# Cross-attention and FP4 feed-forward: heads times values, then a projection of 256 rows, instead of values folded with the output weights

## The chip, the core and the metric

The kernel runs on one NeuronCore of a Trainium2 chip. The core has five engines with a queue each: TensorE (PE, matmuls and transposes into PSUM), VectorE (DVE), ScalarE (ACT), GpSimd (POOL) and SyncE (SP, which only issues DMAs here). An engine works through its queue in order, and waits on semaphores for the others. The metric is the device time in microseconds of one execution; a profiled execution gives the trace.

## What is computed

x is 2 x 1024 x 256, the context 2 x 154 x 256. A layer norm, cross-attention with 16 heads of 64, a layer norm and a gated feed-forward of width 704 whose weights and inputs are rounded to FP4 in blocks of 16:

```python
q = einsum('bnd,hdk->bhnk', layernorm(x), proj_q) + bias_q
k = einsum('bnd,hdk->bhnk', ctx, proj_k) + bias_k
v = einsum('bnd,hdv->bhnv', ctx, proj_v) + bias_v
attn = softmax(einsum('bhqk,bhnk->bhqn', q, k) / sqrt(64))
heads = einsum('bhqn,bhnv->bhqv', attn, v)
x = x + transpose(heads, (0, 2, 1, 3)).reshape(2, 1024, 1024) @ w_out.T
u = layernorm(x)
x = x + fp4_linear(silu(fp4_linear(u, w_gate)) * fp4_linear(u, w_up), w_down)
```

## The kernel before

A product is done with halves: each operand is a float16 `high` and the float16 rest, `low`, and `three` (L349) issues three matmuls, high x high, high x low and low x high. So nearly every PSUM tile that is to be an operand is rounded by ScalarE (high) and then subtracted by VectorE (low).

**Setup.** It loads and splits the projections, makes keys (`J_K` jobs), w_out transposed (`J_WO`) and values (`J_V`, `heads_out`), the latter as a block-diagonal matrix of head pairs, and then folds values with the output weights: 20 `J_VW` jobs (`fold`, evicted by `vw_high` and `vw_low` L870). The result `vw` has for each batch and each row of (head, context position), 16 x 154 = 2464 rows in 20 chunks of 128, the 256 output columns. Among these jobs stand the queries and scores of the first tile, the row statistics and the layer norm of tiles 1 to 7.

**Attention.** There are 8 steps; step i treats rows 128 i to 128 i + 127 of both batches, s = 0 and 1 being the batch. `attention(i)` is written for each engine as a loop over s and five slots g, and that order is the queue. In a slot TensorE scores four heads of the next tile (`score`, L443, for g below 4), transposes 512 columns of the probabilities of this tile (`turn_p`, L451, four fp32 transposes), does one of the side jobs (transposes of the next step's normalised x, L413; one of four query blocks `query(n, j)`, in slots 2 to 4 of the first tile and slot 1 of the second), and multiplies a transposed group with `vw` (`mix`, 12 matmuls of 256 columns, L351 to L353 from vw). VectorE does in a slot the row maximum (L925), the inverse of the row sums (L930), the low half of the transposed probabilities (L934), and the low half of a query (L916); ScalarE the exps (L672), the high half (L682) and that of a query (L663); GpSimd scales the probabilities (L1155). All query blocks from step 1 on share the PSUM bank `Q_BANK`, so a block waits for the low half of the one ahead (`q_low`). One group's mix of a tile into `O_BANK` starts when the sum of the tile before has been read (`x1_ready`). `add_attention` (L942) adds the tile's sum to xs and takes its statistics (L828).

In steps 0 to 5 a sixth of the FFN's weights is rounded to FP4 too: block scales (L951 to L955, second tile, slot 0, VectorE), values (L1161, L1163, GpSimd), magnitudes (L741, ScalarE, slot 3), two grid operations (L984, L986, VectorE, slot 4), and a last product on GpSimd (L1186). In step 7 the weights are transposed (`turn_weights`), and x of the first FFN step is quantised.

**FFN.** Eight steps of two tiles: gate and up (24 matmuls of 352 columns per tile), silu, hidden (L1072), quantising over VectorE, GpSimd and ScalarE, transposes, and the down projection. It is the same before and after.

## Time and profile before

| | us |
|---|---|
| median of 3 runs (454.4 to 455.08) | 454.61 |
| profiled execution | 453.78 |
| its span | 451.6 |
| start of step 1 of attention | 100.4 |
| steps 1 to 5, each | 30.08 |
| step 6 | 28.2 |
| step 7 up to the sum of its second tile | 23.6 |
| first FFN matmul | 302.67 |

The page gives busy times over the whole span. A step is best read in the windows (busy time of each engine in a stretch) and then in the timeline of one engine, where a bracket behind a row names what the engine waited for. The chain of waits follows the work that ended last back in time; where it changes the engine, one engine released the other. Step numbers are those of the loop; the boundaries in the windows are at VectorE's first row maximum of a step.

### The profile page before, as it was taken

What the parts mean: (1) busy time and instruction counts of PE and PEld (TensorE: products, weight loads), DVE (VectorE), ACT (ScalarE), POOL (GpSimd) and SP (SyncE); (2) the same over time, 40 slices, a digit from 0 to 9 for tenths busy, and PEclk for the clock granted to TensorE, in tenths of its full rate; (3) what the DMA queues carried; (4) which work ended last, traced back from release to release, by engine and by line L of the source; (5) the groups of instructions that cost most, each with busy time, mean ns of one, the idle gap of its engine ahead of it and who ended that gap; (6) DMA issues with size and microseconds to landing.
All of it is one profiled execution on the core that took longest, in us unless ns stands there. A gap on an engine that the chain in (4) does not pass through costs nothing.

```text
span 451.6 us, 9319 instructions
## 1 busy us (share of the span) xinstructions
PE 387.9 (86%) x3581; PEld 306.9 (68%) x3581; DVE 346.3 (77%) x677; ACT 277.4 (61%) x859; POOL 206.9 (46%) x183
## 2 busy tenths in 40 slices
PE   1889759999999999999999999996487797788955
PEld 1568638877878878778788788884256565566744
DVE  2789886777876687678766879778868998998792
ACT  3497757678777876787778767855224435424421
POOL 8250033263353442633535423513557778777841
PEclk9999988999999999999999999999888999999998
DMA  7960000000000000000000000000000000000011
GB/s 240 320 220 1 2 0 1 1 1 1 3 1 2 1 1 3 1 1 2 1 1 1 2 1 2 0 2 0 1 1 1 23 14 12 25 13 12 25 36 35
DMA packets 8426, 11.46 MB, mean 25 GB/s; under 512 B 499, under 2 KB 6335, under 8 KB 8383
## 3 DMA queue, kind: packets, MB, share of 16 engines
q1 hardware_dynamic: 8383, 10.88, 7.5%
q8 instruction: 28, 0.46, 0.4%
q14 instruction: 15, 0.12, 0.1%
HBM read 8.78 MB, written 2.10 MB: 24 GB/s over the span
## 4 chain that ended last, share of the span: by engine, by line
DVE 38%; PE 34%; POOL 10%; ACT 10%; issue 6%; DMA 1%; SPq 0%; POOLq 0%; ACTq 0%; DVEq 0%
PE ps L351 9%; PE ps L353 8%; PE ps L352 8%; POOL arena L1163 4%; PE ps L451 4%; PE ps L443 4%; DVE arena L934 4%; DVE negmax L925 3%; ACT arena L672 3%; DVE arena L984 3%; DVE arena L916 3%; DVE arena L986 3%; DVE vw L870 3%; DVE blk_h L951 2%; DVE arena L1072 2%
## 5 line engine op out<-in xcount | busy, mean ns | idle before, releaser
L1155 POOL TENSOR_TENSOR arena<-arena,rinv 128x616 f32<-128x616 f32 x64 | 77.6, 1213 | 148.6 <-DVE rinv L930 148.6
L351 PE MATMUL ps<-vw,arena 128*128 128x256 f16 (+1 forms) x352 | 98.0, 278 | 12.3 <-DVE arena L823 6.1
L672 ACT ACTIVATE arena<-ps,negmax 128x154 f32<-128x154 f32 x256 | 96.0, 397 | 18.0 <-DVE negmax L925 17.7
L352 PE MATMUL ps<-vw,arena 128*128 128x256 f16 (+1 forms) x352 | 97.8, 278 | 0.0
L353 PE MATMUL ps<-vw,arena 128*128 128x256 f16 (+1 forms) x352 | 97.7, 277 | 0.0
L934 DVE TENSOR_TENSOR arena<-ps,arena 128x512 f16<-128x512 f32 x80 | 54.9, 686 | 18.7 <-ACT arena L682 18.5
L682 ACT ACTIVATE arena<-ps 128x512 f16<-128x512 f32 x80 | 48.5, 606 | 25.2 <-PE ps L451 24.0
L351 PE MATMUL ps<-arena,xnT_h 128*128 128x352 f16 x128 | 41.2, 322 | 18.1 <-DVE xnT_l L994 16.3
L925 DVE TENSOR_REDUCE negmax<-ps 128x4 f32<-128x616 f32 x64 | 50.6, 792 | 6.8 <-PE ps L443 5.6
L672 ACT ACTIVATION_READ_ACCUMULATOR arena<-ps,negmax 128x1 f32 x256 | 55.1, 215 | 0.0
L451 PE MATMUL ps<-ident,arena 128*128 128x128 f32 x320 | 52.1, 286 | 0.0
L351 PEld LDWEIGHTS ps<-vw,arena 128*128 128x128 f16 x352 | 34.8, 99 | 20.3 <-issue 6.3
L443 PE MATMUL ps<-kT_h,arena 64*128 64x154 f16 x512 | 37.1, 231 | 4.9 <-DVE vw L870 4.4
L352 PE MATMUL ps<-arena,xnT_h 128*128 128x352 f16 x128 | 41.1, 321 | 0.0
L353 PE MATMUL ps<-arena,xnT_l 128*128 128x352 f16 x128 | 41.0, 320 | 0.0
L451 PEld LDWEIGHTS ps<-ident,arena 128*128 128x128 f32 x320 | 34.9, 142 | 7.9 <-issue 0.2
L916 DVE SCALAR_TENSOR_TENSOR arena<-ps,biasT,arena 128x256 f16<-128x256 f32 x64 | 27.9, 477 | 15.3 <-ACT arena L663 15.1
L353 PEld LDWEIGHTS ps<-vw,arena 128*128 128x128 f16 x352 | 34.8, 99 | 5.3
L352 PEld LDWEIGHTS ps<-vw,arena 128*128 128x128 f16 x352 | 34.8, 99 | 5.0
L663 ACT ACTIVATE arena<-ps,biasT 128x256 f16<-128x256 f32 x64 | 26.8, 470 | 18.5 <-PE ps L353 18.4
L351 PE MATMUL ps<-arena 128*128 128x256 f16 x96 | 27.3, 284 | 10.5 <-DVE arena L1106 9.8
L351 PE MATMUL ps<-xnT_h,wq_h 128*128 128x256 f16 x128 | 35.0, 274 | 0.7
(135 smaller groups left out, 903.7 us busy)
## 6 DMA issues: line engine op xcount, KB each, us to landing
out_dram<-arena SPq DMA_DIRECT2D x16, 128.0 KB, 1.7
xs<-in_x_dram SPq DMA_DIRECT2D x2, 896.0 KB, 10.0
arena<-in_L_xattn_w_out_dram SPq DMA_DIRECT2D x1, 1024.0 KB, 6.3
wffn<-in_L_ffn_w_down_dram SPq DMA_DIRECT2D x1, 704.0 KB, 7.9
wffn<-in_L_ffn_w_gate_dram SPq DMA_DIRECT2D x1, 640.0 KB, 11.0
wffn<-in_L_ffn_w_up_dram SPq DMA_DIRECT2D x1, 640.0 KB, 5.5
vw<-in_ctx_dram SPq DMA_DIRECT2D x1, 308.0 KB
xs<-in_x_dram SPq DMA_DIRECT2D x2, 128.0 KB, 4.9
```

The costliest lines, as they stand in the source:

```text
L351: pe.matmul(o, a_h, b_h, start=start, stop=False)
L352: pe.matmul(o, a_h, b_l, start=False, stop=False)
L353: return pe.matmul(o, a_l, b_h, start=False, stop=stop)
L443: last = pe.matmul(ps[:, 2 * (j % 2) + u, k * L:(k + 1) * L], q[r, p, s * P:(s + 1) * P], kt[r, s, p], start=n == 0, stop=n == 2)
L451: last = pe.transpose(ps[:, T_BANK + (s + g) % 2, k * P:(k + 1) * P], prob[:, s, g * 512 + k * P:g * 512 + (k + 1) * P], ident[:, :])
L663: last = act.activation(q_h[:, 2 * j + k], ps[:, q_bank(i, j), k * 256:(k + 1) * 256], ACT.Identity, bias=biasT[:, 2 * j + k:2 * j + k + 1])
L672: last = act.activation(prob[:, s, h * L:(h + 1) * L], ps[:, 2 * (j % 2) + k % 2, (k // 2) * L:(k // 2 + 1) * L], ACT.Exp, bias=negmax[:, ...
L682: act.activation(pT[:, 0, g, :], ps[:, T_BANK + (s + g) % 2, :], ACT.Copy).then_inc(pt_high, 1)
L916: last = dve.scalar_tensor_tensor(q_l[:, 2 * j + k], ps[:, q_bank(i, j), k * 256:(k + 1) * 256], biasT[:, 2 * j + k:2 * j + k + 1], q_h[:, ...
L925: dve.tensor_reduce(negmax[:, s, 4 * j:4 * j + 4].rearrange("p (k u) -> p u k", k=2), v, AX.X, ALU.max, negate=True).then_inc(max_done, 1)
L934: dve.tensor_tensor(pT[:, 1, g, :], ps[:, T_BANK + (s + g) % 2, :], pT[:, 0, g, :], ALU.subtract).then_inc(pt_low, 1)
L1155: pool.tensor_tensor(v, v, rinv[:, s, 4 * j:4 * j + 4].unsqueeze(2).to_broadcast([P, 4, L]), ALU.mult).then_inc(normed, 1)
```

## The change

Values are no longer folded with w_out. They are kept as `v_h`, `v_l` (128 context positions of a batch x 1024) and, for the other 26 positions, as `vl_h`, `vl_l`, where four heads share 128 rows. `prob` is transposed head by head (16 chunks of 128, L = 154 cut at 128) and the rests of 26, padded to 32, in four more; GpSimd's scaling writes the rests into `rests` in an instruction of its own. `heads(i, j)` multiplies four heads' values with the transposed probabilities of both tiles (24 matmuls of 256 columns, half of them into PSUM partitions 0 to 63, half into 64 to 127); the result is split into `hidT_h`, `hidT_l`, and `project(i, part)` multiplies it with w_out transposed, 48 matmuls in three parts. Both use `O_BANK` alone, in the order `O_ORDER`, each job after VectorE has read the one before (`o_done`). `heads` of step i - 1 stand in step i in the slots `HEADS`, its projection in slots 2 to 4 of the second tile, its sum into xs (`add_attention(i - 2)` seen from step i) at the start of the step after. A step's two tiles are now neighbours in one batch: steps 0 to 3 are of batch 0. Step 0 does w_out's transposes and the values in `O_BANK`. Behind step 7 come its heads and projection, ahead of the FFN. The layer norm of the FFN's first six steps moves from step 6 to step 7. The loads are in another order, in four parts for x, and bias_v is added by matmuls with a row of ones.

```diff
+        O_ORDER = [("wo", n) for n in range(PAIRS // 2)]
+        O_ORDER += [("v", b, n) for b in range(B) for n in range(3)]
+        O_ORDER += [(kind, i, j) for i in range(STEPS) for kind, n in (("pv", QUADS), ("proj", 1)) for j in range(n)]
+        O_AT = {j: n for n, j in enumerate(O_ORDER)}
+        O_HIGH_AT = {j: n for n, j in enumerate(j for j in O_ORDER if j[0] != "proj")}
...
+        HEADS = ((0, 0), (0, 1), (0, 4), (1, 0))
...
             load_proj("k", proj_k, ld_k)
+            for v in range(2):
+                sp.dma_start(xs[:, v, 0], x[0, rows_of(0, v)]).then_inc(ld_x0, 16)
+            load_proj("q", proj_q, ld_q)
             for b in range(B):
-                sp.dma_start(xs[:, b, 0], x[b, 0:P]).then_inc(ld_x0, 16)
+                pairs = x[b].rearrange("(i v p) d -> v p i d", v=2, p=P)
+                first = 1 if b == 0 else 0
+                for v in range(2):
+                    sp.dma_start(xs[:, v, b * STEPS // B + first:(b + 1) * STEPS // B], pairs[v, :, first:]).then_inc(ld_x, 16)
+            load_proj("v", proj_v, ld_v)
+            sp.dma_start(bv_raw, bias_v.rearrange("o h z k -> o (h z k)")).then_inc(ld_bv, 16)
             sp.dma_start(raw["o"].rearrange("p (r n) -> p r n", r=KC),
                          w_out.rearrange("(r p) n -> p r n", p=P)).then_inc(ld_o, 16)
-            load_proj("v", proj_v, ld_v)
-            for b in range(B):
-                sp.dma_start(xs[:, b, 1:], x[b, P:N].rearrange("(i p) d -> p i d", p=P)).then_inc(ld_x, 16)
-            load_proj("q", proj_q, ld_q)
...
+            def next_o(job):
+
+                wait(pe, o_done, O_AT[job])
+                return ps[:, O_BANK, :]
+
...
+            def values(b, n):
+                o = next_o(("v", b, n))
+                for c in range(KC):
+                    three(o, cT_h[:, c, b * L:b * L + P], cT_l[:, c, b * L:b * L + P],
+                          wv_h[:, c, n * 512:(n + 1) * 512], wv_l[:, c, n * 512:(n + 1) * 512], c == 0, False)
+                pe.matmul(o, ones[:, :], bv_h[:, n * 512:(n + 1) * 512], start=False, stop=False)
+                pe.matmul(o, ones[:, :], bv_l[:, n * 512:(n + 1) * 512], start=False, stop=True).then_inc(o_mm, 1)
+
...
+            def heads(i, j):
+
+                b = batch(i)
+                if j == 0: pe.wait_ge(pt_low, GROUPS * (2 * i + 2))
+                o = next_o(("pv", i, j))
+                parts = ((v_h, vl_h, 0), (v_l, vl_l, 0), (v_h, vl_h, 1))
                 for k in range(2):
-                    c = 2 * j + k
-                    o = bank(n)[:, k * D:(k + 1) * D]
-                    heads = pairs_of(c)
-                    for p in heads:
-                        last = three(o, vbd_h[:, p % 2, b, c * P:(c + 1) * P], vbd_l[:, p % 2, b, c * P:(c + 1) * P],
-                                     wot_h[:, p], wot_l[:, p], p == heads[0], p == heads[-1])
-                last.then_inc(job_mm, 1)
+                    for n, (vh, vr, part) in enumerate(parts):
+                        for u in range(2):
+                            h = 4 * j + 2 * k + u
+                            pe.matmul(o[u * DK:(u + 1) * DK, k * 256:(k + 1) * 256], vh[:, b, h * DK:(h + 1) * DK],
+                                      pT[:, i % 2, part, h], start=n == 0, stop=False)
+                        for u in range(2):
+                            last = pe.matmul(o[u * DK:(u + 1) * DK, k * 256:(k + 1) * 256], vr[:, b, j, 2 * k + u],
+                                             pT[:, i % 2, part, H + j], start=False, stop=n == 2)
+                last.then_inc(o_mm, 1)
+
+            def project(i, part):
+                if part == 0:
+                    pe.wait_ge(o_done, O_AT[("pv", i, QUADS - 1)] + 1)
+                    next_o(("proj", i, 0))
+                todo = [(s, p) for s in range(2) for p in range(PAIRS)]
+                for s, p in todo[16 * part // 3:16 * (part + 1) // 3]:
+                    last = three(ps[:, O_BANK, s * D:(s + 1) * D], hidT_h[:, p, s * P:(s + 1) * P],
+                                 hidT_l[:, p, s * P:(s + 1) * P], wot_h[:, p], wot_l[:, p], p == 0, p == PAIRS - 1)
+                if part == 2: last.then_inc(o_mm, 1)
 
             def turn_x(i):
 
                 pe.wait_ge(xn_ready, i + 1)
                 wait(pe, q_low, QUADS * i)
-                v = xn[:, :, :].rearrange("p s (d c) -> p s c d", c=KC)
+                v = xn.rearrange("p s (d c) -> p s c d", c=KC)
                 for c in range(KC):
                     for s in range(B):
...
-            def mix(i, s, g):
-
-                if g == 0:
-                    wait(pe, x1_ready, 2 * i + s)
-                pe.wait_ge(pt_low, GROUPS * (2 * i + s) + g + 1)
-                for k in range(4):
-                    c = 4 * g + k
-                    last = three(ps[:, O_BANK, 0:D], pT[:, 0, g, k * P:(k + 1) * P], pT[:, 1, g, k * P:(k + 1) * P],
-                                 vw[:, s, c, 0:D], vw[:, s, c, D:2 * D], c == 0, c == CHUNKS - 1)
-                last.then_inc(mixed, 1)
 
             def turn_weights(jobs):
 
@@ -497,37 +566,28 @@
 
                         if not exists(ni): turn_weights(jobs_of(g))
 
-                        if g > 0:
-                            mix(i, s, g - 1)
-                        elif exists(shift(i, s, -1)[0]):
-                            mix(*shift(i, s, -1), GROUPS - 1)
+                        if i == 0: first_o(s, g)
+                        if i > 0 and (s, g) in HEADS: heads(i - 1, HEADS.index((s, g)))
+                        if i > 0 and s == 1 and g >= 2: project(i - 1, g - 2)
...
                     if exists(turned[0]): turn_h(*turned)
 
+            heads(STEPS - 1, 0)
             turn_xq(0, 0)
-            mix(STEPS - 1, 1, GROUPS - 1)
+            heads(STEPS - 1, 1)
             pe.wait_ge(wt_low, W1_JOBS)
             turn_xq(0, 1)
-            pe.wait_ge(x1_ready, 2 * STEPS)
+            heads(STEPS - 1, 2)
+            heads(STEPS - 1, 3)
+            for part in range(3):
+                project(STEPS - 1, part)
+            pe.wait_ge(o_done, len(O_ORDER))
...
+                        if i == 0: o_high_part(O_ORDER[GROUPS * s + g])
+                        if i > 0 and (s, g) in HEADS: o_high_part(("pv", i - 1, HEADS.index((s, g))))
...
-            def add_attention(i, s):
-
-                t = 2 * i + s + 1
-                xv = xs[:, s, bass.ds(i, 1), :].rearrange("p o d -> p (o d)")
-                dve.wait_ge(mixed, GROUPS * t)
-                dve.scalar_tensor_tensor(xv, ps[:, O_BANK, 0:D], 1.0 / VW_SCALE, xv, ALU.mult, ALU.add).then_inc(x1_ready, 1)
-                dve.wait_ge(x1_ready, t)
-                row_stats(s, i).then_inc(stats_done, 1)
-
-
+                dve.tensor_tensor(quad_T(1, i, s, g), ps[:, T_BANK + (s + g) % 2, :].rearrange("p (c n) -> p c n", c=4),
+                                  quad_T(0, i, s, g), ALU.subtract).then_inc(pt_low, 1)
+
+            def add_attention(i):
+                job = ("proj", i, 0)
+                dve.wait_ge(o_mm, O_AT[job] + 1)
+                xv = xs[:, :, i]
+                dve.scalar_tensor_tensor(xv, ps[:, O_BANK, :].rearrange("p (s d) -> p s d", s=2), OUT, xv,
+                                         ALU.mult, ALU.add).then_inc(o_done, 1)
+                dve.wait_ge(o_done, O_AT[job] + 1)
+                for s in range(2):
+                    row_stats(s, i).then_inc(stats_done, 1)
 
             def block_scales(src, r, done, t):
...
-                if k == 1:
-                    stats_of(QUADS + 2)
-                    stats_of(QUADS + 3)
-                if 0 <= k - 2 < 2 + NEWTON:
-                    if k == 2: dve.wait_ge(stats_done, 2 * STEPS)
-                    layernorm(1, STEPS, LN_STEPS, [k - 2])
+            for i in range(4, STEPS):
+                stats_of(i)
+            dve.wait_ge(bv_high, 1)
+            dve.scalar_tensor_tensor(bv_l, bv_raw, WS, bv_h, ALU.mult, ALU.subtract).then_inc(bv_low, 1)
+            inverse(0, 0, 0)
+            row_max(0, 0, 2)
+            inverse(0, 0, 1)
+            row_max(0, 0, 3)
+            inverse(0, 0, 2)
+            dve.wait_ge(stats_done, 2 * STEPS)
+            layernorm(1, STEPS, LN_STEPS)
             inverse(0, 0, 3)
             dve.wait_ge(ld_ffn, 80)
             steps(dve, attention, last=W_STEPS)
+            add_attention(STEPS - 2)
+            o_low_part(("pv", STEPS - 1, 0))
             xq_low(0, 0)
-            add_attention(STEPS - 1, 1)
+            o_low_part(("pv", STEPS - 1, 1))
+            xq_low(0, 1)
+            o_low_part(("pv", STEPS - 1, 2))
             scales_x(1)
-            xq_low(0, 1)
+            o_low_part(("pv", STEPS - 1, 3))
+            add_attention(STEPS - 1)
 
             def hidden(i, s):
                 t = 2 * i + s
```

TensorE, a step's first tile, from slot 3 to slot 4, before: the last rows of the mix, the transposes (L451), and the next query block's first row.

```order
L351 MATMUL ps<-vw,arena 128x256
L352 MATMUL ps<-vw,arena 128x256
L353 MATMUL ps<-vw,arena 128x256
L451 MATMUL ps<-ident,arena 128x128 [waits pt_low,normed]
L451 MATMUL ps<-ident,arena 128x128 x3
L351 MATMUL ps<-xnT_h,wq_h 128x256 [waits q_low]
```

The same place after:

```order
L386 MATMUL ps<-xnT_h,wq_h 128x256
L387 MATMUL ps<-xnT_l,wq_h 128x256
L388 MATMUL ps<-xnT_h,wq_l 128x256
L532 MATMUL ps<-ident,arena 128x128 [waits pt_low,normed]
L532 MATMUL ps<-ident,arena 128x128 x3
L386 MATMUL ps<-xnT_h,wq_h 128x256 [waits q_low]
```

Ahead of the transposes stand the query block's own matmuls instead of the mix; the mix is gone.

VectorE, from slot 4 of the second tile into the next step, before: L984 and L986 are the grid operations, L925 a row maximum, L934 the low half of the probabilities, L942 the sum.

```order
L984 SCALAR_TENSOR_TENSOR arena<-wtmp,arena 128x704 [waits wmagic]
L986 SCALAR_TENSOR_TENSOR arena<-wtmp,arena 128x704 [waits wsummed]
L925 TENSOR_REDUCE negmax<-ps 128x2x2 [waits scored]
L934 TENSOR_TENSOR arena<-ps,arena 128x512 [waits pt_high]
L942 SCALAR_TENSOR_TENSOR xs<-ps,xs 128x256 [waits mixed]
L828 BN_STATS stats<-xs 128x6 [waits x1_ready]
```

After: L1036 and L1038 are the grid operations, L994 the sum of both tiles, L940 the low half of heads.

```order
L1036 SCALAR_TENSOR_TENSOR arena<-arena 128x704 [waits wmagic]
L1038 SCALAR_TENSOR_TENSOR arena<-arena 128x704 [waits wsummed]
L978 TENSOR_REDUCE negmax<-ps 128x2x2 [waits scored]
L994 SCALAR_TENSOR_TENSOR xs<-ps,xs 128x2x256 [waits o_mm]
L887 BN_STATS stats<-xs 128x6 [waits o_done]
L887 BN_STATS stats<-xs 128x6
L987 TENSOR_TENSOR pT<-ps,pT 128x4x128 [waits pt_high]
L940 TENSOR_TENSOR arena<-ps,arena 128x512 [waits o_high]
```

The sum stands ahead of the low half (L987), is of both tiles, and has both tiles' statistics and a low half of heads behind it.

VectorE between the last low half of the probabilities (L934, L987) and the FFN, before:

```order
L934 TENSOR_TENSOR arena<-ps,arena 128x512 [waits pt_high]
L965 SCALAR_TENSOR_TENSOR arena<-ps,arena 128x512 [waits wt_high]
L965 SCALAR_TENSOR_TENSOR arena<-ps,arena 128x384 [waits wt_high]
L994 SCALAR_TENSOR_TENSOR xnT_l<-ps,xnT_h 128x2x128 [waits xqt_high]
L942 SCALAR_TENSOR_TENSOR xs<-ps,xs 128x256 [waits mixed]
L828 BN_STATS stats<-xs 128x6 [waits x1_ready]
```

After (L994 sums, L940 low halves of heads, L1046 low halves of the quantised x, L1003 to L1007 block scales):

```order
L994 SCALAR_TENSOR_TENSOR xs<-ps,xs 128x2x256 [waits o_mm]
L887 BN_STATS stats<-xs 128x6 [waits o_done]
L887 BN_STATS stats<-xs 128x6
L940 TENSOR_TENSOR arena<-ps,arena 128x512 [waits o_high]
L1046 SCALAR_TENSOR_TENSOR xnT_l<-ps,xnT_h 128x2x128 [waits xqt_high]
L940 TENSOR_TENSOR arena<-ps,arena 128x512 [waits o_high]
L1046 SCALAR_TENSOR_TENSOR xnT_l<-ps,xnT_h 128x2x128 [waits xqt_high]
L940 TENSOR_TENSOR arena<-ps,arena 128x512 [waits o_high]
L1003 TENSOR_REDUCE blk_x<-arena 128x32 [waits xnormed,xq_done]
L1005 TENSOR_SCALAR blk_x<-blk_x 128x32 [waits xscaled]
L1007 RECIPROCAL blk_x<-blk_x 128x32 [waits xscaled]
L940 TENSOR_TENSOR arena<-ps,arena 128x512 [waits o_high]
```

Four low halves of heads and a second sum stand there now, each behind TensorE and ScalarE.

## Rows read from the trace of the kernel before

**Rows 1.** The page, busy us (share of the span) and instructions of each engine.

```profile
PE 387.9 (86%) x3581; PEld 306.9 (68%) x3581; DVE 346.3 (77%) x677; ACT 277.4 (61%) x859; POOL 206.9 (46%) x183
```

**Rows 2.** Windows: us, busy of each engine with (x instructions), PEclk, DMA share, GB/s.

```profile
100.40:130.46 30.06, 29.05 (x311) 23.77 (x309) 22.30 (x45) 22.97 (x86) 12.64 (x11) 1.00 0.01 2
...
250.80:279.00 28.20, 27.57 (x292) 22.91 (x291) 23.08 (x58) 21.24 (x83) 11.09 (x9) 1.00 0.01 2
```

**Rows 3.** Timeline of TensorE, step 5: start, us, engine line op out<-in xcount [idle <-releaser].

```profile
222.38 0.28 PE L351 MATMUL ps<-vw,arena 128*128 128x256 f16 x1 [0.54 <-DVE xs L942]
...
229.92 0.27 PE L351 MATMUL ps<-vw,arena 128*128 128x256 f16 x1
...
231.23 0.60 PE L451 MATMUL ps<-ident,arena 128*128 128x128 f32 x4
231.92 0.28 PE L351 MATMUL ps<-xnT_h,wq_h 128*128 128x256 f16 x1
...
235.16 0.66 PE L451 MATMUL ps<-ident,arena 128*128 128x128 f32 x4
235.65 0.27 PE L351 MATMUL ps<-vw,arena 128*128 128x256 f16 x1
...
252.46 0.28 PE L351 MATMUL ps<-vw,arena 128*128 128x256 f16 x1 [0.54 <-DVE xs L942]
```

**Rows 4.** Timelines of ScalarE and VectorE, between the two query blocks of rows 3.

```profile
230.12 0.84 ACT L663 ACTIVATE arena<-ps,biasT 128x256 f16<-128x256 f32 x2 [0.71 <-PE ps L353]
...
230.99 0.88 DVE L916 SCALAR_TENSOR_TENSOR arena<-ps,biasT,arena 128x256 f16<-128x256 f32 x2 [0.86 <-ACT arena L663]
```

**Rows 5.** The chain of waits, end of step 5: start us, us, what.

```profile
242.39 1.21 POOL arena L1155
...
243.90 1.40 POOL arena L1163
...
248.11 0.69 DVE arena L934
...
249.87 0.89 DVE arena L986
...
252.07 0.34 DVE xs L942
```

**Rows 6.** The page's groups: ScalarE's exps and its rounding of the probabilities.

```profile
L672 ACT ACTIVATE arena<-ps,negmax 128x154 f32<-128x154 f32 x256 | 96.0, 397 | 18.0 <-DVE negmax L925 17.7
...
L682 ACT ACTIVATE arena<-ps 128x512 f16<-128x512 f32 x80 | 48.5, 606 | 25.2 <-PE ps L451 24.0
```

**Rows 7.** DMA issues, and the chain of waits in the setup.

```profile
arena<-in_L_xattn_w_out_dram SPq DMA_DIRECT2D x1, 1024.0 KB, 6.3
...
16.00 0.17 DVE ln L863
...
20.20 4.24 POOL arena L1145 x2
...
65.83 0.19 DVE ln L863
...
67.99 0.57 PE ps L443 x12
```

**Rows 8.** Timelines of TensorE and VectorE, step 7 and the first FFN tile.

```profile
280.95 0.28 PE L351 MATMUL ps<-vw,arena 128*128 128x256 f16 x1
...
297.94 0.27 PE L451 MATMUL ps<-ident,arena 128*128 128x128 f32 x1
...
302.67 0.32 PE L351 MATMUL ps<-arena,xnT_h 128*128 128x352 f16 x1 [0.30 <-DVE xs L942]
...
307.80 0.88 DVE L1072 SCALAR_TENSOR_TENSOR arena<-ps,arena 128x704 f32<-128x704 f32 x1
```

**Rows 9.** Windows with TensorE's granted clock (PEclk), behind short gaps and one long.

```profile
62.00:64.00 2.00, 1.81 (x9) 1.32 (x10) 1.79 (x10) 0.87 (x2) 0.00 (x0) 0.50 0.00 0
...
314.00:318.00 4.00, 1.49 (x10) 0.99 (x11) 3.69 (x13) 0.84 (x2) 0.00 (x0) 1.00 0.02 4
```

345 lines of the change are left out of this document (174 added, 171 removed).

## The prediction

> **What bounds the kernel now.** I read the page first: TensorE is busy 86% of the span, VectorE 77%, ScalarE 61% [rows 1]. Shares over a span of three stages decide little, so I cut the span into stages next. The attention steps 1 to 5 are equal, 30.08 us each, and in one TensorE is busy 29.05, ScalarE 22.97, VectorE 22.30 us; step 6, which has no FFN weights to quantise, takes 28.20 [rows 2]. Nearly full TensorE suggests that TensorE sets the pace. The timeline of one step says something finer [rows 3]. From the step's mix at 222.38 to the transposes at 235.16 TensorE runs almost without a gap: 12.78 us. From there to the next step's same mix at 252.46 are 17.30 us, and here the chain of waits leaves TensorE: VectorE's steps, the scaling on GpSimd, the block values on GpSimd, exps on ScalarE, then on VectorE the low half of the probabilities, the two grid operations, a row maximum, a low half, and the sum into xs for which TensorE stands still [rows 5]. So a step is a ring through in-order queues. TensorE's mixes fill the ring's waits; they are only half of its length. That is the question for this change: it takes matmuls out, and moves those that are left.
>
> A slot (one g) costs TensorE: 12 matmuls of 256 columns, 229.92 to 231.23, so 1.31 us or 0.109 each; scores 0.62 before the transposes at 235.16, transposes 0.49 behind them to 235.65, together 1.1 [rows 3]. Transposes alone I take at 0.44. A query block ends its issue at 229.92 and the next query block starts at 231.92: 2.00 us, since both use one bank, and between them lie ScalarE's two roundings and VectorE's two subtractions [rows 3, 4]. Before, transposes (0.44) and a mix (1.31) stood between, and the wait left over was 0.25.
>
> **Part 1, TensorE's work.** A step loses 120 matmuls of the mix: 13.1 us. It gains 96 matmuls of heads times values, each 64 output rows wide, in neighbouring pairs for the two halves of the partitions, and 48 of the projection: 5.2 us. If the pairs run side by side, the 96 cost 48 x 0.109 = 5.2 us, and four heads blocks cost 4 x 1.40 with the change of tile shape, which I read as 0.09 off the scores' slot. Side by side is what scores do, 12 matmuls of 154 columns in 0.6 us where one after the other would be 12 x 154 / 2.4 = 0.77 us, but these share rows, not columns, so it is no proof [rows 3]. From below: 5.2 us; from above, one after the other, 10.5. I take 5.2, since the scores are the only rows of two tiles in the array. TensorE then needs about 2.3 us less per step.
> The Trainium skill speaks against such pairs (TensorEngine Tiling (Array Packing), Restrictions): column tiling turns off the fast weight load. Its page TensorE: Matmul & The Clock Gate, LDWEIGHTS, gives columns / 1.2 GHz, an estimate of 53 ns for 64 columns, 107 for a pair, which would still just hide; no row of before shows a column-tiled load. By that rule a pair stays at 0.109 if loads hide and doubles if they don't.
>
> **Part 2, the first half of the ring.** I walk a step in the order of each queue, with a four-head exps block 1.46 (four of 0.397 that overlap little, the readings between them), a 128x512 rounding 0.61 and 0.69 for the subtraction behind it [rows 5, 6]. Time 0 is the first heads block. Heads 0 ends at 1.35, slot 1's scores and transposes at 2.44, x transposes 2.88, heads 1 (it waits for its bank: 0.2 + 0.63 + 0.69 after heads 0) 4.35, slot 2 to 5.44, query 0 to 6.78. Now the change shows: no mix stands in slots 2 and 3. Query 1 would be ready at 7.87 but its bank is free 2.0 us after query 0, at 8.86 with ScalarE's exps in the way: wait 1.0. Query 2 has 0.44 of transposes as cover: wait 1.56. Query 2 ends at 13.48, heads 2 at 14.90, and the transposes of the second tile stand at 15.5 instead of 12.78. **+2.7 us.** The cover that mixes gave is gone, and what was saved on TensorE is idle time.
>
> **Part 3, the second half.** VectorE has one more 0.69 subtraction (heads 3) there, and one for two sums instead of two (0.36 each before, 0.69 now), statistics of both tiles behind it; heads 3 waits 0.5 for heads 2's bank. The scaling on GpSimd becomes two instructions; I take +0.1 for the second. The low half that stood between the row maximum and the sum moves behind it, -0.6 [rows 5]. Sum +0.4 +0.1 -0.6 +0.3: 17.5 instead of 17.30. TensorE's own work there, heads 3, two queries' worth and the three thirds of the projection, is some 13 us, so it isn't late. A step is 15.5 + 17.5 = 33.0: +2.9. **Steps 1 to 5: +14.6.** Bounds: -2.3 (TensorE sets the pace) to +5.5 (the pairs aren't side by side) a step.
> Step 6, without the weights' chain: first half the same, then TensorE's own slots, 14.8: 30.3 instead of 28.5, **+1.8**. Step 7 now holds the layer norm of the first six steps that stood in step 6 (some 4 us of VectorE), o-bank subtractions and a wait for the normalised x; from its first mix at 280.95 to the last transposes at 297.94 are 16.99 [rows 8]; I walk it to 21.8: **+4.8**, bounds 0 to 7.
>
> **Part 4, the setup.** The folding of values with the output weights goes: 20 jobs, which fill the time from 24.5 to 67.99 with the value heads; TensorE's first score of step 0 in the second tile stands at 67.99, and the last layer norm operation that ScalarE waits for at 65.83 [rows 7]. After: proj_q is third in the queue, where the 1 MB of w_out took 6.3 us, so it lands near 12 us, before it is wanted. GpSimd makes its low half in 4.24 us, as that of proj_v before, from 20.2 to 24.5 [rows 7]. Four query blocks in two banks, the first 1.31 and then 2.0 each pair, end on VectorE at 32.7. Then in a row: scaling of proj_v 1.1, rounding 2.0, the bias 1.0, three exps blocks to 41.5, and the layer norm of seven tiles whose 19 operations of 0.17 follow each other only [rows 7]: 3.3 us, to 45.0. Before, that layer norm was sliced into other work; now it is all in a row, and last. So step 0 starts 22 to 23 us earlier. It holds the values' work (4 groups of transposes, 4 blocks of 8 matmuls of 512 columns, two of the rest): ScalarE and VectorE have ten more pairs of operations in it, so I take 36 us for it where steps take 33. First heads block at 45 + 36 = 81, where the first mix of step 1 stood at 252.46 - 5 x 30.08 = 102.06: **-21**, bounds -26 and -15.
>
> **Part 5, behind the last step.** Before, from the last transposes at 297.94 to the first FFN matmul at 302.67 are 4.73 us [rows 8]. Now all four heads blocks of step 7 and its projection come after, in one bank. Last third of the projection before it to 3.0, sum and start at 3.9; then three times 1.40 + 0.2 + 0.63 + 0.69 + 0.05 = 2.97, the fourth block the same to 15.8, 48 projections of 0.109 to 21.05, the sum of 0.69 to 22.05. **+17.3**, bounds +14 and +23. The x quantising of step 1 and the table load hide there, so the first hidden layer comes 4.55 after the first FFN matmul instead of 5.2 (307.80 less 302.67): **-0.65** [rows 8]. The FFN stage behind is as it was, and where its chain is VectorE it stays VectorE.
>
> **Sum.** -21 + 14.6 + 1.8 + 4.8 + 17.3 - 0.65 = +16.9 us. The profiled execution took 453.78, of which 451.6 is the span; with the sum it is 470.7. The median of the runs, 454.61, is 0.83 above the profiled one: **471.5 us**.
>
> **Rivals.**
> - A, faster: TensorE sets the pace after all, and the waits of queries and of the sum find cover. For it: 29.05 of 30.06 busy [rows 2]. Against it: nothing is left in slots 2 and 3 to fill 2.0 us. It decides from the point where a step is under 29.2. Then -2.3 in each of seven steps (-16), -23 to step 1, +16.7 at the end: about 432 us. The setup's gain alone would carry it.
> - B, heads' pairs run one after the other: +1.3 us for each block, four in the ring, five steps and two, and at the tail: +39. About 510 us.
> - C, TensorE's clock falls in the new waits. TensorE is idle 3.8 us before each first heads block, and half of the tail. Before, gaps of 1 to 1.5 us with a microsecond's work between ended at 1.2 GHz (62 to 64), while a gap of 3.3 in front of 316.5 did not (314 to 318) [rows 9]. Price 1.5 us in a step and 5 at the end: about 484.
> - D, waits are covered by half, since my walk leaves out overlap of neighbouring operations: 1.6 us less a step, 460 us.
> - E, that the fold isn't gone or the order isn't as read: the order of instructions shows both, so it gets nothing.
>
> **How the numbers follow.** Forecast 0.50 (464 to 480), D 0.14 (452 to 464), C 0.17 (to 491), B 0.10, A 0.09. The range leaves out B and A: 452 to 491. A measurement of this kernel tells some 0.2% from no change. A and a small part of D are faster: 0.11; within 0.2%: 0.02; slower 0.87.
>
> **What would show it.** The step's length in the windows: 33 us confirms parts 2 and 3, under 29.2 confirms A. Waits of about 1.0 and 1.5 us of a query matmul for a VectorE subtraction, once each per step. 3 to 4 us of TensorE idle before the first heads block, released by the sum into xs. 24 heads matmuls in 1.4 us (pairs) or 2.7 (B). First heads block of step 1 at 81 us. 22 us from the last attention transposes to the first FFN matmul. Granted clock below 1.00 in the steps would be C. It is wrong if the walk missed a queue that hides the query waits, or if the first step starts later than 49 us.

## The result: slower by 7.9%, and where the time went

| | before | changed |
|---|---|---|
| median, us | 454.5 (4 runs, 453.71 to 455.08) | 490.29 (4 runs, 489.6 to 490.76) |
| profiled execution, us | 453.78 | 490.69 |
| its span, us | 451.6 | 488.9 |

The ratio is 1.0788, with a 95% interval of 1.0765 to 1.081. The direction was forecast; the size was not. Forecast were +16.9 us, measured are +35.8 in the medians and +37.3 in the spans. Cut at the places that the prediction names, in us of the profiled executions:

| stretch | before | forecast | changed | clock kept up |
|---|---|---|---|---|
| start to step 0 (ScalarE normalises x of step 1) | | 45.0 | 48.65 | 45.27 |
| step 0, to the first heads block of step 1 | 102.06 (both) | 36 | 41.72 | 39.98 |
| steps 1 to 5 | 150.4 | 165.0 | 175.70 | 166.13 |
| step 6 | 28.49 | 30.3 | 31.87 | 30.35 |
| step 7, to the last attention transposes | 16.99 | 21.8 | 22.34 | 44.49 (both) |
| to the first FFN matmul | 4.73 | 22.05 | 22.15 | |
| FFN | 148.93 | 148.28 | 146.47 | 148.28 |
| span | 451.6 | 468.4 | 488.9 | 474.5 |

The last column is the profile of an experiment, told below, in which matmuls that nobody reads keep TensorE's granted clock up in most of its waits and nothing else is changed. Put beside the forecast it is the short answer: it is 6 us off the forecast, 4 of them in step 0, and the changed kernel is 14 us more than it. In three of the runs below some executions fell in a slower state, and the medians given are those of the others.

First the page of the changed kernel: its busy line, the clock in 40 slices of the span, and one group; rows 1 are those of before.

```profile
PE 376.1 (77%) x3659; PEld 287.5 (59%) x3659; DVE 356.2 (73%) x677; ACT 278.2 (57%) x868; POOL 210.4 (43%) x248
...
PEclk9985897599899899898899999899988899999999
...
L468 PE MATMUL ps<-pT,v_h 128*64 128x256 f16 x256 | 38.7, 306 | 31.0 <-DVE xs L994 21.3
```

TensorE's busy time fell by 12 us while the span grew by 37 [rows 1]: work was taken off the engine with the highest share, and the step was not bound by it. The L468 row says where TensorE stands: 31.0 us idle before heads matmuls, 21.3 of them until VectorE's sum into xs. The clock row (9 is full speed) has 14 of 40 at 8 or below.

The windows, in the form of rows 2, for step 0, steps 1 to 5, step 6, step 7, the stretch behind it, and the FFN:

```profile
48.65:90.37 41.72, 31.94 (x281) 19.26 (x281) 29.91 (x58) 31.49 (x105) 15.23 (x21) 0.82 0.00 1
90.37:266.07 175.70, 143.65 (x1660) 117.04 (x1661) 125.54 (x235) 123.38 (x450) 69.53 (x97) 0.94 0.01 2
266.07:297.94 31.87, 28.33 (x333) 23.15 (x334) 21.93 (x43) 22.99 (x87) 10.90 (x17) 0.95 0.01 1
297.94:320.28 22.34, 18.59 (x210) 15.02 (x210) 19.58 (x49) 16.06 (x51) 7.80 (x11) 0.92 0.01 2
320.28:342.43 22.15, 15.47 (x179) 12.84 (x178) 9.36 (x19) 7.39 (x14) 1.30 (x2) 1.00 0.01 1
342.43:488.90 146.47, 112.34 (x808) 81.74 (x808) 118.70 (x189) 54.31 (x101) 89.69 (x80) 0.96 0.04 15
```

PEclk is the third number from the right: 0.82 in step 0, 0.94 in steps 1 to 5, where steps of before had 1.00 [rows 2]. 0.94 of 175.7 us looks like little. It is not little if the slow stretch stands on the ring. The timeline of TensorE in step 4, as rows 3, from its first heads block:

```profile
195.74 0.42 PE L468 MATMUL ps<-pT,v_h 128*64 128x256 f16 x2 [3.88 <-DVE xs L994]
195.93 0.45 PE L471 MATMUL ps<-pT,vl_h 128*64 128x256 f16 x2
...
198.44 0.25 PE L522 MATMUL ps<-kT_h,arena 64*128 64x154 f16 x2
...
200.01 0.30 PE L468 MATMUL ps<-pT,v_h 128*64 128x256 f16 x2
200.15 0.28 PE L471 MATMUL ps<-pT,vl_h 128*64 128x256 f16 x2
...
201.45 0.24 PE L522 MATMUL ps<-kT_h,arena 64*128 64x154 f16 x2
...
205.82 0.28 PE L386 MATMUL ps<-xnT_h,wq_h 128*128 128x256 f16 x1 [0.76 <-DVE arena L969]
...
209.15 0.28 PE L386 MATMUL ps<-xnT_h,wq_h 128*128 128x256 f16 x1 [1.41 <-DVE arena L969]
...
213.49 0.30 PE L468 MATMUL ps<-pT,v_h 128*64 128x256 f16 x2 [0.32 <-DVE arena L940]
```

Each row is a pair of matmuls. In the second block, from 200.01, pairs follow each other in 0.109 us and the block takes 1.44 to the scores behind it. In the first block, behind 3.88 us of idle TensorE, the same pairs take 0.21 and the block 2.70: 1.2 instead of 2.4 GHz, and the granted clock from 195.74 to 197.74 is 0.50. The forecast waits are there too: 3.88 before the first block, 0.76 and 1.41 before the second and third queries, 0.32 for the heads' bank.

The tail is as forecast, one bank and four blocks 2.92 us apart (324.48, 327.40, 330.31, 333.24), 17.95 us from the first block to the first FFN matmul at 342.43, where 18.15 were worked out. The first hidden layer comes at 347.01, 4.58 us behind it; 5.13 before [rows 8], 4.55 forecast.

### The profile page after: what moved, and what is told of

Its sections match the earlier page's. It is cut to its first block, busy times and chain, and to the rows that moved or that the text cites. A ratio compares the mean times of both kernels' runs of the same rounds, so it can differ in the third digit from the quotient of the medians.

```text
span 488.9 us, 9450 instructions
## 1 busy us (share of the span) xinstructions
PE 376.1 (77%) x3659; PEld 287.5 (59%) x3659; DVE 356.2 (73%) x677; ACT 278.2 (57%) x868; POOL 210.4 (43%) x248
## 4 chain that ended last, share of the span: by engine, by line
PE 37%; DVE 31%; ACT 17%; POOL 8%; issue 4%; DMA 1%; SPq 0%; POOLq 0%; DVEq 0%; ACTq 0%
PE ps L386 7%; PE ps L388 6%; PE ps L387 6%; ACT arena L727 6%; PE ps L468 6%; PE ps L471 5%; DVE arena L969 4%; POOL arena L1215 4%; ACT arena L718 3%; DVE arena L1036 3%; ACT arena L713 3%; DVE negmax L978 3%; PE ps L532 2%; DVE arena L1038 2%; ACT pT L736 2%
## 5 line engine op out<-in xcount | busy, mean ns | idle before, releaser
L1207 POOL TENSOR_TENSOR arena<-arena,rinv 128x104 f32<-128x104 f32 x64 | 23.1, 361 | 155.1 <-DVE rinv L983 155.1
L987 DVE TENSOR_TENSOR pT<-ps,pT 128x512 f16<-128x512 f32 x80 | 54.9, 687 | 16.8 <-ACT pT L736 16.4
L1208 POOL TENSOR_TENSOR arena<-arena,rinv 128x512 f32<-128x512 f32 x64 | 66.7, 1042 | 0.0
L468 PE MATMUL ps<-pT,v_h 128*64 128x256 f16 x256 | 38.7, 306 | 31.0 <-DVE xs L994 21.3
L736 ACT ACTIVATE pT<-ps 128x512 f16<-128x512 f32 x80 | 50.3, 629 | 7.5 <-PE ps L532 7.5
L386 PE MATMUL ps<-arena 128*128 128x256 f16 (+2 forms) x120 | 36.6, 305 | 19.6 <-DVE arena L1159 9.8
L713 ACT ACTIVATE arena<-ps 128x512 f16<-128x512 f32 x32 | 19.1, 598 | 57.2 <-PE ps L471 57.2
L940 DVE TENSOR_TENSOR arena<-ps,arena 128x512 f16<-128x512 f32 x32 | 21.8, 680 | 25.0 <-ACT arena L713 24.9
L522 PEld LDWEIGHTS ps<-kT_h,arena 64*128 64x128 f16 x512 | 24.2, 101 | 25.6 <-issue 20.4
L468 PEld LDWEIGHTS ps<-pT,v_h 128*64 128x64 f16 x256 | 16.6, 119 | 38.3 <-issue 28.1
L471 PE MATMUL ps<-pT,vl_h 128*64 128x256 f16 x256 | 38.4, 301 | 0.0
```

Source lines behind the costliest of these rows:

```text
L386: pe.matmul(o, a_h, b_h, start=start, stop=False)
L468: pe.matmul(o[u * DK:(u + 1) * DK, k * 256:(k + 1) * 256], vh[:, b, h * DK:(h + 1) * DK], pT[:, i % 2, part, h], start=n == 0, stop=False)
L471: last = pe.matmul(o[u * DK:(u + 1) * DK, k * 256:(k + 1) * 256], vr[:, b, j, 2 * k + u], pT[:, i % 2, part, H + j], start=False, stop=n == 2)
L522: last = pe.matmul(ps[:, 2 * (j % 2) + u, k * L:(k + 1) * L], q[r, p, s * P:(s + 1) * P], kt[r, batch(i), p], start=n == 0, stop=n == 2)
L736: act.activation(quad_T(0, i, s, g), ps[:, T_BANK + (s + g) % 2, :].rearrange("p (c n) -> p c n", c=4), ACT.Copy).then_inc(pt_high, 1)
L987: dve.tensor_tensor(quad_T(1, i, s, g), ps[:, T_BANK + (s + g) % 2, :].rearrange("p (c n) -> p c n", c=4), quad_T(0, i, s, g), ALU.subtrac ...
```

## Experiments

Each run is one change to the changed kernel. The kernel before ran beside them, at medians of 453.92 to 455.35 us, and a ratio is to that.

### TensorE's clock

The first run fills the wait at a step's start, so that the clock can't fall there:

```diff
+            def fill(i):
+                wait(pe, q_low, QUADS * min(i + 1, STEPS))
+                for _ in range(16):
+                    pe.matmul(ps[:, Q_BANK, :], wq_h[:, 0, 0:P], wq_h[:, 0, 0:512], start=True, stop=True)
...
+                        if 2 <= i <= 6 and s == 0 and g == 0: fill(i)
                         if i > 0 and (s, g) in HEADS: heads(i - 1, HEADS.index((s, g)))
```

> Sixteen matmuls of 512 columns are added on TensorE in front of the first heads block of steps 2 to 6, into the bank of the queries, whose contents are not used; they fill 3.4 us of the 3.88 us in which TensorE stands still for the sum into xs. Nothing else changes. Theory C (the clock falls in that gap, and the heads block behind it, 195.74 to 198.44, takes 2.70 us instead of 1.40, on the chain): the block takes 1.40 again, five steps are 1.3 shorter each, total -6.5, 483.8 us. Rival (TensorE's slow start is hidden, since ScalarE and VectorE wait for exps anyway): under 1 us in all, 489.5 to 490.5 us.

Measured: 483.24 us (ratio 1.0625, 1.059 to 1.0661), 7.05 less. The timeline of step 4, and the window of steps 2 to 5:

```profile
187.42 3.62 PE L559 MATMUL ps<-wq_h 128*128 128x512 f16 x16
191.45 0.30 PE L468 MATMUL ps<-pT,v_h 128*64 128x256 f16 x2 [0.41 <-DVE xs L1000]
...
125.05:257.85 132.80, 121.26 (x1393) 93.60 (x1393) 99.58 (x189) 98.22 (x360) 55.62 (x79) 1.00 0.01 2
```

TensorE still waits for the same sum; it only does something meanwhile. The block behind takes 1.43 us, and the four steps take 132.80 / 4 = 33.20 us each, all equal. In the changed kernel they took 34.75, 34.82, 34.49 and 35.84, so 1.3 to 2.6 us more. The low clock doesn't always end with the first block. In step 4 it lasts 2.7 us, to the scores at 198.44, and costs 1.3; in step 5 it lasts 5.8 us, from 230.23 into the second block, and costs 2.6. About half of the slow stretch comes back as length of the step each time, and the forecast of the walk, 33.0, is near for a kernel whose clock stays up.

The next does the same in step 0: ten such matmuls in the 2.3 us wait before the third values block, and fourteen in front of step 1.

> Ten matmuls of 512 columns in TensorE's 2.3 us wait before the third block of values in step 0 and fourteen in the wait before the first heads block of step 1, into the bank of the queries. Theory (TensorE's clock, 0.69 of full in the last 18 us of step 0, lengthens it): 3 us of the 5.7 come back, first heads block near 87.5 us, total 487. Rival (the clock costs nothing there, ScalarE and VectorE set the pace of step 0): under 1 us.

Measured: 487.12 us (1.0724, 1.0686 to 1.0763), 3.2 less. Step 0 is 85.54 - 46.05 = 39.49 us instead of 41.72, so 2.2 come back there and not 3, and step 1 goes from 35.80 to 33.20, which I hadn't counted. These two make 4.8 us in the profile where the medians show 3.2; the total of 487 was met with other terms than mine. The first heads block came at 85.54 and not near 87.5 because ScalarE began step 0 at 46.05 in this execution and not at 48.65; that is told under the setup.

Then all places together, also in the setup: twenty short matmuls before the key projections, ten in the wait for w_q's low half, twenty-four between the second and third scores.

> Matmuls whose results nobody reads stand in TensorE's waits, in banks that are free then: twenty before the key projections, ten in the wait for the low half of w_q, twenty-four between the second and third scores of the setup, ten and fourteen in step 0 and in front of step 1, sixteen in front of steps 2 to 6. Theory (of the 20.4 us by which the changed kernel is over the forecast, 16.3 are TensorE at half clock: 2.9 in the setup, 2.2 in step 0, 2.6 in step 1, 7.1 in steps 2 to 5, 1.5 in step 6): 490.3 - 16.3 = 474 us, steps of 33.2, within 3 us of the forecast of 471.5. Rival (these add up to less, since the engines behind take the time back, or the added matmuls hold the queue): 480 us or more.

Measured over five rounds: 474.96 us (1.0452, 1.0426 to 1.0478), 15.3 less, where 16.3 were expected. Its windows, cut as those above, and its clock row:

```profile
45.27:85.25 39.98, 34.49 (x304) 20.72 (x305) 29.91 (x58) 31.50 (x105) 15.23 (x21) 0.91 0.00 1
85.25:251.38 166.13, 151.58 (x1740) 116.93 (x1741) 124.68 (x235) 122.97 (x450) 69.56 (x97) 1.00 0.01 2
251.38:281.73 30.35, 26.87 (x334) 21.88 (x334) 21.77 (x43) 22.95 (x87) 10.90 (x17) 1.00 0.01 2
281.73:326.22 44.49, 32.60 (x387) 26.93 (x387) 28.94 (x67) 23.28 (x65) 9.10 (x13) 1.00 0.00 1
326.22:474.50 148.28, 114.41 (x808) 83.29 (x808) 118.69 (x189) 54.32 (x101) 89.68 (x80) 0.94 0.04 15
...
PEclk9998799999999999999999999999878999999998
```

VectorE and ScalarE are as busy in these stretches as in the changed kernel, to 1 us in 125: no work went away. What went is TensorE at half clock, though not all of it: step 0 still shows 0.91, with a low stretch from 47 to 54. This run also settles the FFN, which took 146.47 us in the changed kernel's profile and 148.28 here. Cut at VectorE's sixth and last block maximum of the hidden layer, the middle part is 78.22 us in both. The first and the last part of the changed kernel, then of this run:

```profile
342.43:389.49 47.06, 34.66 (x214) 23.10 (x215) 36.70 (x76) 16.67 (x33) 24.37 (x22) 0.89 0.00 1
...
467.71:488.90 21.19, 11.57 (x98) 9.27 (x96) 13.41 (x15) 4.95 (x9) 6.09 (x7) 0.99 0.11 38
...
326.22:374.06 47.84, 35.57 (x214) 23.66 (x215) 36.70 (x75) 16.68 (x33) 24.47 (x22) 0.86 0.00 1
...
452.28:474.50 22.22, 12.71 (x98) 10.27 (x96) 13.41 (x15) 4.95 (x9) 6.10 (x7) 0.91 0.10 36
```

The 1.8 us lie where the granted clock differs, 0.8 in the first part and 1.0 in the last, with the same matmuls and the same busy VectorE. The kernel before took 48.51, 78.17 and 22.25 us for the three parts: against this run the forecast gain is in the first part, 0.67 us.

### The first half of a step: query waits

The second and third heads blocks go between the query blocks, where the mixes had stood:

```diff
-        HEADS = ((0, 0), (0, 1), (0, 4), (1, 0))
+        HEADS = ((0, 0), (0, 2), (0, 3), (1, 0))
```

> The second and third heads blocks stand in slots 2 and 3 of a step's first tile, between the query blocks, instead of in slots 1 and 4, on TensorE, ScalarE and VectorE. My part 2 (the query waits of 0.81 and 1.41 us are lost cover, and lie on the path): both go under 0.2 us, the first half of the ring falls by 2.0, total -14, 476 us. Rival (ScalarE's queue sets that half, the waits only show where its lateness is seen): waits go, but the step is shortened by under 0.7, total over 485.

Measured: 485.52 us (1.0682, 1.0617 to 1.0747), 4.8 less and not 14; steps 2 to 5 take 137.00 us, 34.25 each. The query waits are gone, the wait before the first block has grown to 4.36. Since the clock falls behind that one, I put both edits together, with eighteen added matmuls for sixteen, as the wait is longer:

> The second and third heads blocks between the query blocks, and eighteen matmuls of 512 columns in front of the first heads block of steps 2 to 6, which keep the clock up. With the added matmuls alone a step was 33.20 us, with the heads blocks alone 34.2. If the query waits (2.2 us) are on the path once the clock is out of it: 31.2, total 471 us. Rival (ScalarE's queue sets the first half, the query waits are slack behind it): 32.6 to 32.9, total 480 us.

Measured: 479.36 us (1.0551, 1.0512 to 1.0591). The window of steps 2 to 5, and from the chain of waits the part in which step 4 loses what its first half gained:

```profile
124.60:256.32 131.72, 123.11 (x1400) 94.47 (x1401) 99.28 (x189) 98.37 (x360) 55.63 (x79) 1.00 0.01 2
...
206.06 0.88 DVE arena L975 x2
206.93 0.70 DVE negmax L984
207.64 0.60 DVE pT L993
208.23 0.80 DVE blk_w L1009
...
209.71 0.55 DVE arena L946
```

32.93 us a step against 33.20 with the queries waiting: 2.17 us of waits were worth 0.27. The fourth heads block comes 15.20 us after the first instead of 16.47, so the first half did shrink by 1.27; a microsecond of it is given back at once, because VectorE is then the link from 206 to 213, working through its queue without a gap, the block scales of the weights (L1009) in the middle of it. So the waits were real, forecast to 0.25 us, and nearly slack. The rival's size came, but the chain names VectorE's queue and not ScalarE's. The clock, on the other hand, did not forgive the wait of 4.36: 34.25 against 32.93.

### The sum's place

Where do the 3.88 us before the first heads block come from? Two runs say. In one the heads blocks move away from it, HEADS = ((0, 1), (0, 2), (0, 3), (0, 4)):

> All four heads blocks in the slots 1 to 4 of a step's first tile, so that the first scores, transposes and the x transposes of the step no longer stand behind the sum into xs. If the 3.9 us wait for the sum, the half clock behind it (1.3) and the query waits (2.2) are what the chain holds: 5 us a step less, steps of 30, total 490 - 35 = 455 us. Rival (the ring is closed by VectorE's and ScalarE's own queues, exps and the weights' chain, and TensorE's waits only move): 2 us a step, 476 us.

Measured: 466.87 us (1.0264, 1.0216 to 1.0313), 23.4 less, between the two. Steps 2 to 5 take 122.82 / 4 = 30.70 us. In the other nothing moves on TensorE, and only the sum moves on VectorE:

```diff
-                        if s == 0 and g == 0 and i >= 2: add_attention(i - 2)
...
+                        if s == 1 and g == 4 and i >= 1: add_attention(i - 1)
                         if w and g == 4:
                             dve.wait_ge(wmagic, i + 1)
                             minus_grid((wtmp[0], None, wtmp[1]), wsummed, wgrid, i)
```

> The sum of a step's projection into xs, with its statistics, stands on VectorE at the end of the same step, ahead of the two grid operations of the weights, instead of behind them and a row maximum; nothing moves on TensorE. Theory (the 3.88 us wait is the sum's place in VectorE's queue, and all of it is on the ring): the wait falls under 0.7, the clock stays up, 4.8 us a step less, 461 us. Rival (ring closed by the row maximum, the next exps and the heads rounding ahead of them on ScalarE; the sum's 1.4 us now delay that row maximum): wait gone too, but 2.3 us a step, 475 us.

Measured: 473.69 us (1.0399, 1.0361 to 1.0436), 16.6 less; steps of 126.78 / 4 = 31.70. Its timeline of TensorE:

```profile
150.79 0.30 PE L468 MATMUL ps<-pT,v_h 128*64 128x256 f16 x2 [1.05 <-DVE xs L994]
155.11 0.30 PE L468 MATMUL ps<-pT,v_h 128*64 128x256 f16 x2 [1.25 <-DVE arena L940]
```

The 3.88 became 1.05, the clock stayed at full speed (1.00 over steps 2 to 5), and a new 1.25 appeared one block later. That, and the size, fit the rival's mechanism, a row maximum and exps now behind the sum and the grid operations. Against the 33.20 us of a step with its clock kept up, moving the sum is worth 1.5 and moving the blocks 2.5. In the run with the blocks moved, where the clock stayed at 1.00 as well, VectorE's queue at a step's end reads so:

```profile
207.94 1.27 DVE L1036 SCALAR_TENSOR_TENSOR arena<-arena 128x704 f32<-128x704 f32 x1
209.24 0.89 DVE L1038 SCALAR_TENSOR_TENSOR arena<-arena 128x704 f32<-128x704 f32 x1
210.05 0.79 DVE L978 TENSOR_REDUCE negmax<-ps 128x4 f32<-128x616 f32 x1
210.76 0.68 DVE L994 SCALAR_TENSOR_TENSOR xs<-ps,xs 128x512 f32<-128x512 f32 x1
```

The two grid operations of the weights stand in front of the row maximum for which ScalarE waits 2.12 us. By this reading they close the ring. No run moves them alone; the version further below moves them with the rest of the weights' chain, and its steps are 29.42 us.

### The setup and step 0

Two changes in the setup: the scaling and rounding of proj_v and the value bias stand among the query blocks, and the layer norm is cut into slices. The code below shows the second.

```diff
+            dve.wait_ge(stats_done, 2 * STEPS)
+            layernorm(1, STEPS, LN_STEPS, [0, 1])
             inverse(0, 0, 0)
             row_max(0, 0, 2)
+            layernorm(1, STEPS, LN_STEPS, [2])
             inverse(0, 0, 1)
             row_max(0, 0, 3)
+            layernorm(1, STEPS, LN_STEPS, [3])
+            layernorm(1, STEPS, LN_STEPS, [4])
             inverse(0, 0, 2)
-            dve.wait_ge(stats_done, 2 * STEPS)
-            layernorm(1, STEPS, LN_STEPS)
             inverse(0, 0, 3)
```

> Only the setup: scaling and rounding of proj_v and of the value bias stand among the query blocks instead of behind them, and the layer norm's 19 operations are cut into slices between the first row maxima. Theory (step 0 started 3.6 us later than forecast because these stood in one row: 1.2 scaling, 2.0 and 1.04 rounding, 2.5 bias, 4.8 layer norm): ScalarE normalises the x of step 1 at 42 to 43 us instead of 48.65, total -6, 484 us. Rival (TensorE's w_q low half and the exps set it): -2 or less, 488 us.

Measured: 483.18 us (1.0616, 1.0598 to 1.0633), 7.1 less; ScalarE starts step 0 at 41.64. But the reference point of that expectation, 48.65, is not a fixed number. Ten profiles have a setup with the same instructions, and the start is at 45.36 to 46.05 in six of them and at 47.76 to 48.94 in four, the changed kernel's among them. A window of the changed kernel, over the first query blocks, shows the larger part of the difference, the clock:

```profile
24.00:28.00 4.00, 3.82 (x20) 2.81 (x21) 2.00 (x7) 0.84 (x2) 0.12 (x1) 0.57 1.09 371
```

In the run with the sum moved the same window reads 1.00, and its queries are 2.9 us earlier at the end. Of these, 1.3 were there before the first query (22.91 against 24.18): the 308-column matmuls of the key projections follow each other in 0.26 us up to 17.4 in the changed kernel and up to 15.0 in the other, and in 0.13 from there, half and full pace, though PEclk reads 1.00 there in both. So the order in a row costs 4 us (45.7 against 41.64), and the other 3 are TensorE at half pace.

Step 0 itself is 41.60 to 42.12 us in seven profiles. What is in it that I had not priced?

> Step 0 without its two blocks for the values of key positions 128 to 153 (32 narrow matmuls, four roundings of 26 partitions on ScalarE and four subtractions on VectorE each); those values stay zero, so that part of the attention is left out. Theory (step 0 is 5.7 us longer than I forecast because each of these blocks holds its bank 3.3 us more than a common one, 0.8 matmul, 1.5 and 1.7 us of rounding and subtraction, and the 2.3 and 2.9 us waits of TensorE behind them): first heads block of step 1 at 84 us instead of 90.4, total -6, 484 us. Rival (they are covered, the excess is elsewhere): -2 or less.

Measured: 479.54 us (1.0568, 1.0525 to 1.061), 10.7 less. The first heads block of step 1, and ScalarE's first normalisation, in this run:

```profile
78.06 0.30 PE L469 MATMUL ps<-pT,v_h 128*64 128x256 f16 x2 [1.78 <-DVE pT L988]
...
45.98 0.60 ACT L767 ACTIVATE arena<-xs,ln 128x256 f32<-128x256 f32 x1 [3.42 <-DVE ln L923]
```

The first block of step 1 comes 32.08 us after ScalarE's start, 9.64 less: without the two small blocks step 0 is no longer than an ordinary step. Their rows in the changed kernel, ScalarE then VectorE:

```profile
85.77 1.53 ACT L708 ACTIVATE vl_h<-ps 26x256 f16<-26x256 f32 x4
...
88.51 1.72 DVE L935 TENSOR_TENSOR vl_l<-ps,vl_h 26x256 f16<-26x256 f32 x4
...
90.37 0.42 PE L468 MATMUL ps<-pT,v_h 128*64 128x256 f16 x2 [2.86 <-DVE vl_l L935]
```

26 partitions of 128 in each operation, and 0.4 us for each, as for 128 partitions of as many columns (0.38 on ScalarE and 0.41 on VectorE for 128x256 in the tail): four of them where a common block has one of 0.60 and one of 0.69. And since TensorE waits behind them (2.30 and 2.86 us), they also bring its clock down: of the 9.6 us some 2 are that, by the run which fills those waits.

### Pairs in the array

> In a heads block a head's six matmuls of 64 columns of weights come in a row, then the other head's, so that neighbours no longer stand in different halves of the columns. If the halves run side by side only as neighbours (theory of part 1): 24 matmuls take 2.6 instead of 1.4 us, 1.2 for each of 32 blocks, those in the second half of a step partly covered: 490 + 25 to 39 = 515 to 529 us. Rival (the order does not matter to the array): 490 us and blocks of 1.4.

Measured: 497.29 us (1.092, 1.0895 to 1.0945), 7.0 more, and not 25 to 39. The timeline of one block, from 200.66, with the scores behind it:

```profile
200.66 0.30 PE L469 MATMUL ps<-pT,v_h 128*64 128x256 f16 x1
200.80 0.27 PE L470 MATMUL ps<-pT,vl_h 128*64 128x256 f16 x1
200.91 0.27 PE L469 MATMUL ps<-pT,v_l 128*64 128x256 f16 x1
200.91 0.30 PE L469 MATMUL ps<-pT,v_h 128*64 128x256 f16 x1
...
202.34 0.24 PE L520 MATMUL ps<-kT_h,arena 64*128 64x154 f16 x2
```

Within a head the matmuls are 0.11 apart. But the second head's first one, seventh in the program, starts at 200.91, beside the first head's third. So the halves of the columns do run side by side, and they need not be neighbours: the block takes 1.68 us instead of 1.44. Both my theory and my rival fail in size; 32 blocks of 0.24 us more make 7.7. Rival B's price of 1.3 a block would have needed an array that does not do this at all. The Trainium skill, TensorEngine Tiling (Array Packing), Key Properties, says that different tiles can load weights and multiply in parallel; the trace agrees, and shows 0.24 us more a block for pairs that stand six instructions apart.

### The end

The last four heads blocks write the banks of the scores instead of one bank, and TensorE waits for the turned FFN weights ahead of the first block and no longer ahead of the third:

```diff
-                o = next_o(("pv", i, j))
+                o = ps[:, j, :] if i == STEPS - 1 else next_o(("pv", i, j))
```

> The four heads blocks behind the last step write four banks (those of the scores, free by then) instead of one after the other into one. Part 5 of the prediction says that three times 2.92 us is TensorE waiting for its one bank: the blocks then follow each other in 1.4 us, the last subtraction ends some 7.5 us earlier and the stretch from the last attention transposes to the first FFN matmul falls from 22.15 to 14.7 us, total 482.8. Rival (something else in that stretch, the quantising of x or the last weights, is as late): less than 3 us, over 487.

Measured: 487.68 us (1.0733, 1.0703 to 1.0764), 2.6 less. The stretch from the last attention transposes fell from 22.15 to 17.87, and the FFN behind took 148.4 instead of 146.47, the difference explained above. The expectation of 7.5 was too much by its own spacing, since three times 2.92 less three times 1.4 is 4.6. The blocks stand at 323.50, 325.30, 327.18 and 328.52, and the first can't come earlier whatever the banks are: TensorE is busy with the last weights and the projection of step 6 up to it. So of part 5's 17.3 us, 4.3 are the single bank, and the rest is mostly four blocks and 48 projection matmuls that have nothing beside them.

### A version of all changes together

Heads blocks in slots 1 to 4, the weights' chain begun one tile earlier (scales on VectorE in slot 4 of the first tile, grid operations in slot 3 of the second), the setup of above, the last heads blocks in three banks, and the last projection behind the first gate and up matmuls:

> A version with all heads blocks in slots 1 to 4 (as in the run of that change alone), the weights' chain begun in slot 4 of the first tile (scales on VectorE, block values on GpSimd before its scalings, magnitude on ScalarE in slot 1, grid operations in slot 3 of the second tile) instead of at the end, the setup as in the run of that change alone, and at the end the last heads blocks in three banks with the last projection behind the first gate and up matmuls. If the weights' chain is what closes the ring at the end of a step (2.7 us of VectorE waiting for exps behind it, 2.1 of ScalarE waiting for the row maximum behind the grid operations), steps go from 30.7 to about 27.5 us, the setup gives 6 and the end 5: 467 - 19 - 6 - 5 = 437 us, less than the 454 before. Rival (TensorE and VectorE are full in a step by then): steps of 29.5, 449 us.

Measured: 447.29 us, a ratio of 0.9826 (0.9791 to 0.9861) to the kernel before: 1.7% less, small but clear of no change. Two of its steps, 3 and 6:

```profile
147.43:176.85 29.42, 26.83 (x335) 21.88 (x334) 24.70 (x48) 24.55 (x91) 13.64 (x19) 1.00 0.01 2
...
236.71:263.59 26.88, 26.30 (x329) 21.36 (x329) 21.05 (x42) 22.43 (x86) 10.87 (x16) 1.00 0.01 2
```

The step is near the rival's 29.5 us, not 27.5. Step 6, which has no weights' chain, has its 26.88 with TensorE busy 26.30: there TensorE is all but full at last, and the step is 1.6 us shorter than the 28.49 of the kernel before, mix to mix (28.20 by the cut of [rows 2]). But steps 1 to 5 together take 150.75 us where the kernel before took 150.4. The gain lies in step 6 and in front of step 1, where the folding was: the first heads block of step 1 comes at 85.96, 16.1 us before the first mix of the kernel before. Step 7, the stretch behind it and the FFN, which now holds the last projection, give 13.6 of it back. Two attempts at more gave nothing. One put the second grid operation a slot later:

> As the version of all changes together, with the second of the two grid operations one slot later, behind the reciprocals and the low half that exps wait for. Steps were 29.42 at full clock there, with 2.2 us of grid operations ahead of a scaling that GpSimd waits for. Theory: 0.9 us a step less in six steps, 442 us. Rival (it only moves the wait): 447 us.

Measured: 449.27 us (0.9889, 0.9852 to 0.9926). The other filled a wait of 1.85 us, behind which three of its first five steps (1, 2 and 5) ran 3 to 4 us at half clock:

> The version of all changes together, with seven matmuls of 512 columns, read by nobody, in the 1.85 us wait of TensorE for exps in slot 1 of each second tile, behind which two or three of its steps ran partly at half clock (30.4 instead of 29.4 us). Theory: all steps at 29.4, 447.3 - 3 = 444 us. Rival: 447 us.

Measured: 447.53 us (0.9857, 0.9826 to 0.9889). Its profile has steps 2 to 5 at 29.42 and a span of 444.9 instead of 447.8, but the medians don't show it. The intervals of both runs overlap that of the first version, and neither is called a gain or a loss.

## Why the prediction was wrong

Right, with their measures: **part 1** (24 heads matmuls in 1.40; 1.44 to the scores). The loads of 64 columns take 119 ns each in the page of the profile (110 in the median), not the 53 of the prediction's estimate and not less than loads of 128 columns (98 in the median), and yet a pair stays at 0.109 us. So the rule of the Trainium skill that the prediction set against this part (TensorEngine Tiling (Array Packing), Restrictions), that column tiling turns the fast load off, did not lengthen the blocks. **Parts 2 and 3**, the length of a step: 33.0 forecast, 33.20 measured at full clock; step 6: 30.3 and 30.35. **Step 7**: 21.8 and 22.34. **Part 5**: 22.05 and 22.15, though the forecast's last addition is 0.3 above its terms (21.05 and 0.69 are 21.74), and the FFN's -0.65, measured as 4.58 against 5.13 at its first hidden layer.

Wrong, in the order of size:

1. **The clock was taken for a rival and left out of the sum.** It costs 15.3 us in the medians and 14.4 between the two profiles: 9.6 in steps 1 to 5, 1.5 in step 6, 1.7 in step 0 and 3.4 in the setup, less 1.8 by which the FFN is shorter. The failed step is that this term stood at nothing in the sum, by the weighing of rival C. I put two rows side by side, a fall behind gaps of 1 to 1.5 us and no fall behind one of 3.3 [rows 9], and gave C 0.17 and 1.5 us a step. The price of a step was near (1.9 measured on average, 1.3 to 2.6); the chance was not. Of the rows at hand, those of the step itself had TensorE busy 29 of 30 us with a wait of 0.54 [rows 2, 3], and one of 3.8 was, by my own walk, to come back in every step. The same trace also has a fall that the prediction doesn't show, behind a gap of 6.06, with a granted clock of 0.59 from 324 to 328:

   ```profile
   326.55 0.47 PE L351 MATMUL ps<-arena,xnT_h 128*128 128x352 f16 x1 [6.06 <-DVE xnT_l L994]
   ```

   Nor did C price the setup and step 0, where 3.4 of the 3.65 us of late start and 1.7 of the 5.7 in step 0 were the clock, nor did it ask how long a fall lasts. Its total of 484 is the nearest of the forecasts to the measured 490.3, but in part by luck: the 5 us that it puts at the end did not come (the granted clock is 1.00 from 320.28 to 342.43), and 5.1 us in the setup and step 0, which it doesn't price, did.
2. **Step 0 at 36 us was a guess** from "ten more pairs of operations". It was 41.7, and 39.98 with the clock mostly up. The missing term is the two blocks of the rests: 8 roundings and 8 subtractions of 26 partitions that cost as much as those of 128. Without the two blocks step 0 is 32.08, so they cost 9.6 us in all, some 2 of them by the clock, and 36 us had left 4 for them. The term named them ("two of the rest") and did not multiply them out.
3. **Part 2's reason.** "What was saved on TensorE is idle time" and +2.7 us for it: the first half did take 15.5, but the waits were not its price. They do stand on the chain of the run with added matmuls, but with them covered a step is only 0.27 us shorter, since VectorE's queue is then as late in the second half. The number is right; the reason given for it, lost cover, holds only until the next path takes over, which the walk did not look for.
4. The setup's start, 45.0, was right in a kernel whose clock stays up (45.27), though not by its parts. The bias's subtraction took 2.50 us where I had put some of 1.0 for the pair, which is told below.

Rivals: A is excluded by every step. B is excluded by the trace of the changed kernel, and the run of pairs shows that even its mechanism was mis-stated. C is right and is 14 to 15 of the 20 us. D is excluded: the waits stand in full, 0.76, 1.41 and 3.88 us.

What stays open: why the setup keeps its clock in six profiles and loses it in four with the same instructions; and which runs of the changed kernel other than the profiled one lost it (its four runs are within 0.24% of each other).

## What to carry to other kernels

Price a new idle gap of the matmul engine twice, once as the gap and once as the work behind it at half clock, above all if the gap comes back in every round and the work behind it opens the ring. When an in-order walk of all queues gives a step's length, the waits in it are not its cause: cover one alone before calling it the price. And count operations and their columns, not their partitions: four roundings of 26 partitions cost four roundings. Taking work from the busiest engine did not shorten the five equal steps even in the best version (150.75 against 150.4 us); what that version gains (447 against 454 us) comes from step 6 and from the setup and step 0, where the folding was.

## What the runs showed of the hardware

**The clock.** The granted clock is at one of two levels, 1.2 and 2.4 GHz by the 0.21 and 0.109 us of a pair. Behind the 3.88 us gaps it was at the lower in every step, behind 4.36 too, behind 2.32 not in steps 2 to 5 of the run with the blocks moved, behind 1.85 in three of the first five steps of the version of all changes, and behind 1.09 at 311.35 in the changed kernel's step 7. So the length of the last gap alone does not tell it, as in the kernel before, where it was not lower behind 3.29 at 316.51. In step 2 of the changed kernel it fell in the middle of the block, at 126.8, 0.6 us after TensorE had started again. Matmuls that nobody reads, in a bank that is free, hold it in most places: 15.3 us for 158 instructions here. The Trainium skill, TensorE: Matmul & The Clock Gate, HAM oscillation, describes such a case, a wait between bursts that makes every round start at the low clock; the runs with waits of 3.88 and 4.36 us agree, and put its price at 1.3 to 2.6 us in a step of 33.

**VectorE behind GpSimd.** The subtraction of the value bias, one partition of 1024, took 2.50 us in the changed kernel and 1.21 in the run with the setup rearranged. GpSimd's tensor_tensor:

```profile
36.05 4.21 POOL L1199 TENSOR_TENSOR arena<-arena 128x1024 f16<-128x1024 f32 x2 [11.93 <-ACT arena L671]
...
38.84 2.50 DVE L1101 SCALAR_TENSOR_TENSOR pT<-pT 1x1024 f16<-1x1024 f32 x1
```

ends at 40.26, and VectorE's operation 1.1 us later, near its length in the other run. The one of 1.21 us, at 24.40, ran when GpSimd was idle, and a layer norm operation of 14 columns, 0.17 us elsewhere, took 1.08 beside another of GpSimd's (at 44.46). The statistics of 36.22 to 38.8, which read one tensor, were not held. VectorE operations that read two tensors of SBUF seem to wait for GpSimd's to end; no run isolates this, and it is an inference from these rows.

**Two halves of the array** run side by side with up to six instructions of the other half between them (above).
